# Attention over 25 blocks of query rows: each 125-row transposition split into halves of 64 and 61 rows, the two halves copied out by VectorE and ScalarE

## What is computed

```python
x = _layernorm(x + _L0_gnn_ref(x, ..., edge_weight, src, dst, edge_type_8), axis=-1)
x = _layernorm(x + _L1_gnn_ref(x, edge_index, ...), axis=-1)

def _transformer_conv(x, src, dst, Wq, bq, Wk, bk, Wv, bv, Ws, bs, heads):   # heads = 2, C = 64
    q = (x @ Wq + bq).reshape(n, heads, C)
    k = (x @ Wk + bk).reshape(n, heads, C)
    v = (x @ Wv + bv).reshape(n, heads, C)
    alpha = jnp.sum(q[dst] * k[src], axis=-1) / np.sqrt(C)
    ex = jnp.exp(alpha - amax[dst])                    # amax: segment maximum of alpha
    a = ex / denom[dst]                                # denom: segment sum of ex
    out = jax.ops.segment_sum(v[src] * a[..., None], dst, num_segments=n).reshape(n, heads * C)
    return out + x @ Ws + bs
# _L1_gnn_ref: conv with weights 1, ReLU, conv with weights 2
```

## Time and profile before

| | |
|---|---|
| median of 3 runs | 2248.33 us (2247.84 to 2248.36) |
| the profiled execution | 2249.5 us, of which the span of its instructions 2247.5 us |
| granted TensorE clock, mean over the span | 0.981 |
| TensorE matmul busy (PE) | 2104.2 us, 94% of the span |
| TensorE weight load busy (PEld) | 1707.9 us, 76% |
| VectorE (DVE) | 1590.5 us, 71% |
| ScalarE (ACT) | 1291.7 us, 57% |
| GpSimd (POOL) | 821.2 us, 37% |
| attention layer 1, steps | about 1250 to 1711 us |
| attention layer 2, steps | about 1762 to 2240 us |

### The profile page before, as it was taken

The page is one execution under the profiler, slowest core; times in us unless marked ns, Lnnn a source line. Parts: engine busy times, 40 slices in busy tenths (PEclk is TensorE's granted clock), DMA queues, the critical chain, the costliest instruction groups (busy, mean ns, idle before and its releaser), DMA issues. The chain is left out here.

```text
span 2247.5 us, 55086 instructions
## 1 busy us (share of the span) xinstructions
PE 2104.2 (94%) x19640; PEld 1707.9 (76%) x19640; DVE 1590.5 (71%) x4061; ACT 1291.7 (57%) x2303; POOL 821.2 (37%) x1091
## 2 busy tenths in 40 slices
PE   1299999999999999999997999999999999999998
PEld 1288888898888888888985677777776677777776
DVE  1458887888888888878873666666664666666765
ACT  1156666665666666666663555556564455565555
POOL 0766776777677667767710000000000000000000
PEclk9599999999999999999998999999999999999999
DMA  4001111111111111111112222222221122222220
GB/s 122 14 31 45 42 46 51 44 45 52 47 38 46 51 48 41 46 51 44 43 40 100 87 78 72 80 85 85 85 85 48 71 94 92 92 92 92 92 92 7
DMA packets 52538, 141.57 MB, mean 63 GB/s; under 512 B 9261, under 2 KB 43755, under 8 KB 45855
## 3 DMA queue, kind: packets, MB, share of 16 engines
q1 hardware_dynamic: 49804, 129.55, 16.3%
q0 software_dynamic: 2576, 9.68, 1.5%
HBM read 93.95 MB, written 45.27 MB: 62 GB/s over the span
## 5 line engine op out<-in xcount | busy, mean ns | idle before, releaser
L778 PE MATMUL ps<-matrixT,x_rows 125*128 125x256 f32 (+1 forms) x2500 | 582.7, 384 | 2.9 <-ACT aggT L864 2.1
L778 PEld LDWEIGHTS ps<-matrixT,x_rows 125*128 125x128 f32 x2500 | 461.4, 191 | 70.9 <-issue 3.3
L845 ACT COPY matrixT<-ps 125x500 f32<-125x500 f32 (+2 forms) x800 | 395.8, 583 | 201.5 <-PE ps L766 197.3
L1468 ACT COPY weightsT_l<-ps 125x500 f32<-125x500 f32 (+1 forms) x450 | 233.8, 542 | 369.2 <-PE ps L1389 369.2
L766 PE MATMUL ps<-high_weights,low_onehot 64*125 64x125 f32 x6300 | 403.8, 279 | 23.2 <-issue 11.3
L1546 DVE CUSTOM_DVE_ANT_0 scores_l<-ps,bias_rows_l 125x500 f32<-125x500 f32 (+1 forms) x700 | 396.8, 619 | 35.3 <-issue 33.7
L766 PEld LDWEIGHTS ps<-high_weights,low_onehot 64*125 64x125 f32 x6300 | 366.2, 189 | 54.0 <-issue 37.2
L1389 PEld LDWEIGHTS ps<-eye,scores_l 125*125 125x125 f32 x2500 | 301.1, 189 | 115.6 <-issue 97.2
L1389 PE MATMUL ps<-eye,scores_l 125*125 125x125 f32 x2500 | 364.2, 286 | 4.8 <-ACT scores_l L1450 3.4
L1554 DVE COPY weightsT_l<-ps 125x500 f32<-125x500 f32 (+1 forms) x250 | 150.0, 600 | 267.3 <-PE ps L1389 264.9
L1450 ACT ACTIVATE scores_l<-scores_l,neg_max_l 125x1500 f32<-125x1500 f32 x200 | 320.9, 1605 | 20.5 <-DVE neg_max_l L1583 20.4
(11 more groups left out here) (154 smaller groups left out, 1864.5 us busy)
## 6 DMA issues: line engine op xcount, KB each, us to landing
bias_rows_l<-bias SPq DMA_DIRECT2D x50, 1562.5 KB, 6.7
bias<-bias SPq DMA_DIRECT2D x150, 250.0 KB
edges<-rec POOLq DMA_DIRECT2D x1, 2014.2 KB, 11.8
x_rows<-in_x SPq DMA_DIRECT2D x1, 1562.5 KB
bias<-bias SPq DMA_DIRECT2D x25, 62.5 KB
x<-x_rows SPq DMA_DIRECT2D x25, 62.5 KB
x_rows_l<-x SPq DMA_DIRECT2D x25, 62.5 KB
out<-rows_l SPq DMA_DIRECT2D x25, 62.5 KB
```

Of the source, the lines that this page charges most:

```text
L778: last = nc.tensor.matmul(psG[:, BASES * SPLIT * side:BASES * (SPLIT * side + SIDE[side])], x[:, h, :], MT[side][:, 0:SIDE[side], BASES * ...
L845: last = nc.scalar.copy(MT[side][:, at:at + 2 * c - 1:2, 0:COLS], psP[bank][0:R, :].rearrange("p (i c) -> p i c", c=128)[:, 0:c, 0:COLS])
L1468: nc.scalar.copy(PT[i % 8][:, 0:cw[c]], psT[i % 2][0:R, 0:cw[c]]).then_inc(z["pa_ok"], 1)
```

## The change

- The operand of a turn is split by query rows: `QS = ((0, 64), (64, 125))`. Each square becomes two transpositions, one of partitions 0 to 63 into `psT[0]` and one of partitions 64 to 124 into `psT[1]`, both heads of the chunk in each bank.
- `turn(u, up, c)` now turns a whole chunk, both heads. It waits for both exps, and for both copies of the chunk before.
- The first half-square of each chunk is a plain matmul with the identity, not a transposition.
- The copies i = 2c (rows 0 to 63, ScalarE) and i = 2c + 1 (rows 64 to 124, VectorE) both start from the turned chunk: seven on each engine, where it was nine and five. `PT` is four tiles of a chunk each.
- The transposition of the sums and the skip product stand ahead of turn 2, not behind it.
- VectorE alternates masks and copies; `finish` stands behind mask 5; the copy of chunk 5 stands ahead of mask 6; in layer 2 the mean and variance (`moments`) come after the negated maximum and `normalize` a step later.

```diff
-        PT = [sb(f"weightsT{i}", [R, CW], F32) for i in range(8)]
+        PT = [sb(f"weightsT{i}", [R, HEADS, 4, R], F32) for i in range(4)]
-        ON_V = (1, 5, 8, 11, 13)
+        ON_V = (1, 3, 5, 7, 9, 11, 13)
+        QS = ((0, HD), (HD, R))
+        def turned_chunk(eng, u, i):
+
+            c, (lo, hi) = i // HEADS, QS[i % HEADS]
+            k = cw[c] // R
+            eng.wait_ge(z["t_ps"], u * CH + (c + 1))
+            buffer_free(eng, u, i)
+            return (PT[c % 4][:, :, 0:k, lo:hi],
+                    psT[i % HEADS][0:R, 0:HEADS * k * (hi - lo)].rearrange("p (h b q) -> p h b q", h=HEADS, b=k))
-            def turn(u, up, i):
-                c, hd = i // HEADS, i % HEADS
+            def turn(u, up, c):
+
                 if c in (0, EXP_AT):
-                    pe.wait_ge(z["exp_ok"], u * 4 + (hd + 1 + 2 * (c > 0)))
-
-                if i >= 2:
-                    chunk_out(pe, u, i - 2)
-                elif not is_int(u) or u >= 1:
-                    chunk_out(pe, u - 1, i - 2 + NT)
-                for b in range(cw[c] // R):
-                    n = 4 * c + b
-                    last = nc.tensor.transpose(psT[i % 2][0:R, b * R:(b + 1) * R], S[up][:, hd, n * R:(n + 1) * R],
-                                               eye[0:R, 0:R])
+                    pe.wait_ge(z["exp_ok"], u * 4 + (2 if c == 0 else 4))
+
+                for i in (HEADS * c - 2, HEADS * c - 1):
+                    if i >= 0:
+                        chunk_out(pe, u, i)
+                    elif not is_int(u) or u >= 1:
+                        chunk_out(pe, u - 1, i + NT)
+                k = cw[c] // R
+                for hd in range(HEADS):
+                    for b in range(k):
+                        at = (4 * c + b) * R
+                        for side, (lo, hi) in enumerate(QS):
+                            n = hi - lo
+                            to = psT[side][0:R, (hd * k + b) * n:(hd * k + b + 1) * n]
+                            if hd == 0 and b == 0 and side == 0:
+                                nc.tensor.matmul(to, S[up][lo:hi, hd, at:at + R], eye[lo:hi, lo:hi], start=True, stop=True)
+                            else:
+                                last = nc.tensor.transpose(to, S[up][lo:hi, hd, at:at + R], eye[lo:hi, lo:hi])
                 last.then_inc(z["t_ps"], 1)
...
+                if layer == 2 and inside(t - 3):
+                    normalize(t - 3, 1 - par)
                 if inside(t):
                     mask(2)
+                if inside(u):
+                    turned_out(3)
+                if inside(t):
                     mask(3)
                 if inside(u):
                     turned_out(5)
+                if inside(t):
+                    mask(4)
+                if inside(u):
+                    turned_out(7)
+                if inside(t):
+                    mask(5)
                 if inside(w):
                     finish(w, par, then)
-                if inside(t):
-                    mask(4)
-                    mask(5)
                 if inside(u):
-                    turned_out(8)
-                if layer == 2 and inside(w):
-                    normalize(w, par)
+                    turned_out(9)
+                    turned_out(11)
                 if inside(t):
                     mask(6)
...
                     V.tensor_scalar_mul(neg[par][:, :], top[:, :], -1.0).then_inc(z["neg_ok"], 1)
+                if layer == 2 and inside(w):
+                    moments(w, par, then)
                 if inside(u):
-                    turned_out(11)
                     turned_out(13)
```

More of the change, by code:

```diff
@@ L1362, in product @@
                         last = nc.tensor.matmul(psO[up][HD * hd:HD * (hd + 1), 0:R], vals[:, 4 * c + b, hd, :],
-                                                PT[(HEADS * c + hd) % 8][:, b * R:(b + 1) * R],
+                                                PT[c % 4][:, hd, b, :],
                                                 start=(c == 0 and b == 0), stop=(c == CH - 1 and b == 0))
@@ L1400, in step @@
                         product(w, par, CH - 1)
-                    if s > 0 and inside(u):
-                        turn(u, up, 4 * s - 4)
-                        turn(u, up, 4 * s - 3)
                     if s == 2 and inside(w):
@@ L1408, in step @@
                         nc.tensor.matmul(psO[par][0:R, 384:384 + D], x_now[par][:, :], W["s"][:, :], start=True, stop=True).then_inc(z["o_ps"], 1)
+                    if s > 0 and inside(u):
+                        turn(u, up, 2 * s - 2)
                     if s > 0 and inside(t):
@@ L1413, in step @@
                     if s > 0 and inside(u):
-                        turn(u, up, 4 * s - 2)
-                        turn(u, up, 4 * s - 1)
+                        turn(u, up, 2 * s - 1)
                         if s == 1 and (not is_int(u) or u >= 2):
@@ L1424, in step @@
                 if inside(u):
-                    turn(u, up, NT - 2)
-                    turn(u, up, NT - 1)
+                    turn(u, up, CH - 1)
             pipeline_loop(pe, step)
@@ L1464, in step @@
                             continue
-                        c = i // HEADS
-                        act.wait_ge(z["t_ps"], u * NT + (i + 1))
-                        buffer_free(act, u, i)
-                        nc.scalar.copy(PT[i % 8][:, 0:cw[c]], psT[i % 2][0:R, 0:cw[c]]).then_inc(z["pa_ok"], 1)
+                        to, turned_rows = turned_chunk(act, u, i)
+                        nc.scalar.copy(to, turned_rows).then_inc(z["pa_ok"], 1)
                         if layer == 1 and i == 12 and inside(w):
@@ L1513, in finish, with moments @@
                     V.tensor_scalar_max(r[:, :, :], r[:, :, :], 0.0).then_inc(z["rows_ok"], 1)
-                else:
-                    v.wait_ge(x_in[par], (half(w, par) + 1) * 16)
-                    then(V.tensor_tensor(r[:, :, :], r[:, :, :], x_old[par][:, :, :], ALU.add))
-                    then(V.bn_stats(stats[:, 0, :], r[:, 0, :]))
-                    V.memset(spare2[:, :], 0.0).then_inc(then.sem, 1)
-                    then.done = then.done + 1
-                    then(V.bn_aggr(mean[:, 0, :], stats[:, 0, :]))
-                    V.tensor_scalar_add(rstd[:, :, :], mean[:, :, 1:2], 1.0e-5).then_inc(z["asked"], 1)
+            def moments(w, par, then):
+                r = rows[par]
+                v.wait_ge(x_in[par], (half(w, par) + 1) * 16)
+                then(V.tensor_tensor(r[:, :, :], r[:, :, :], x_old[par][:, :, :], ALU.add))
+                then(V.bn_stats(stats[:, 0, :], r[:, 0, :]))
+                V.memset(spare2[:, :], 0.0).then_inc(then.sem, 1)
+                then.done = then.done + 1
+                then(V.bn_aggr(mean[:, 0, :], stats[:, 0, :]))
+                V.tensor_scalar_add(rstd[:, :, :], mean[:, :, 1:2], 1.0e-5).then_inc(z["asked"], 1)
             def normalize(w, par):
@@ L1537, in step @@
                     if not is_int(t) or t >= 2:
-                        v.wait_ge(z["t_ps"], (t - 1) * NT)
+                        v.wait_ge(z["t_ps"], (t - 1) * CH)
                         v.wait_ge(z["neg_ok"], t - 1)
@@ L1550, in turned_out @@
                 def turned_out(i):
-                    c = i // HEADS
-                    v.wait_ge(z["t_ps"], u * NT + (i + 1))
-                    buffer_free(v, u, i)
-                    V.tensor_copy(PT[i % 8][:, 0:cw[c]], psT[i % 2][0:R, 0:cw[c]]).then_inc(z["pt"], 1)
+                    to, turned_rows = turned_chunk(v, u, i)
+                    V.tensor_copy(to, turned_rows).then_inc(z["pt"], 1)
                 if inside(t):
@@ L1583, in step @@
                     V.tensor_scalar_mul(neg[par][:, :], top[:, :], -1.0).then_inc(z["neg_ok"], 1)
+                if layer == 2 and inside(w):
+                    moments(w, par, then)
                 if inside(u):
-                    turned_out(11)
                     turned_out(13)
-            pipeline_loop(v, step)
+            pipeline_loop(v, step, 2 if layer == 1 else 3)
 INPUTS = ['x', 'src', 'dst', 'edge_type_8', 'edge_weight', 'L0_gnn_V', 'L0_gnn_w_comp', 'L0_gnn_loop_w', 'L0_gnn_bias',
```

## The result

The changed kernel takes 2323.92 us (median of four runs, 2321.99 to 2325.05); the kernel before took 2248.35 us beside it. The ratio is 1.0334 (95% interval 1.0316 to 1.0352): 75.6 us slower. The profiled execution of the changed kernel took 2324.1 us with a span of 2322.1; its mean granted clock is 0.970, where it was 0.981. Two versions further down had one execution each that took far longer than their other three (2764.8 us in last_turns_apart, 5295.0 us in all_mended_whole_squares); no reading rests on these two.

A forecast was written before the change was run, and what follows sets the result against it. TensorE was taken as the bound, its work filling the attention step. Plain pass, saved switches and two waits summed to +58.7 us, making the profiled 2249.5 us 2308 and the median 2307; range 2255 to 2350 us, the forecast's own 2285 to 2335.

The forecast's parts named there:

- A half pair costs a whole square: In the turns, two half transpositions side by side take 0.109 us, as one whole square does; gain 0 us.
- Rivals 1 and 4: In turns: 1, streamed columns set the pace, 2190 us, 14%; 4, halves do not overlap, 2580 us, 4%.
- The plain pass: In each of seven chunks, the plain matmul's second pass costs one more load interval, +0.76 us a step.
- Rival 2: In the turns, the plain pass hides: 38 us less than forecast, 2269 us; chance 12%.
- Switches: On TensorE, fewer changes of array division at 0.195 us each: -0.98 us a step in layer 1, -1.17 in layer 2.
- rival 3: Between scores and turns the switch stays: +24 us, 2331 us; chance 7%.
- The wait at turn 5: Between turns 4 and 5, TensorE waits for both banks' copies under only the short chunk's scores, +0.82 us a step.
- The wait at turn 0: Ahead of turn 0, later exponentials (copy ahead of mask 6) hold TensorE: +0.62 us in layer 1, +0.77 in layer 2.
- The sum over the steps: Over both layers' steps, 29.9 us in layer 1 and 28.8 in layer 2, together +58.7 us.
- nothing but at the very end, below 1 us: At the kernel's end, the output's DMA going a step later costs below 1 us, elsewhere nothing.
- 1.9 us of scores or products cover the wait: Away from turn 5, scores or products stand under the wait for both banks' copies; edges costed at 0.

The follow-up runs named there:

- last_turns_apart: Changed kernel with a product between each two turns, from turn 1 on, in each layer's last step with turns; 2329.9 us.
- all_mended_whole_squares: all_mended with whole squares, one head in each bank, in place of the halves; 2266.7 us.
- no_plain: Changed kernel with each chunk's plain matmul made a transposition, the semaphore waits on an instruction of their own; 2295.6 us.
- whole_squares: Changed kernel with whole 125 x 125 squares, one head in each bank, in place of halves; order and waits kept; 2321.4 us.
- m6_first: Changed kernel with mask 6, the maximum and its negation ahead of VectorE's copy of chunk 5 again; 2297.3 us.
- last_step_whole: all_mended with the last step with turns of each layer turned in whole squares, other steps in halves; 2220.6 us.
- m6_first_no_plain: Changed kernel with both mask 6 ahead of the copy of chunk 5 and no plain matmul; 2264.2 us.
- scores5_later: Changed kernel with the scores of chunk 5 moved from behind turn 2 to behind turn 4; 2296.9 us.
- all_mended: Changed kernel with mask 6 first, no plain matmul, product 3 behind turn 4, earlier finish, and the last step of last_turns_apart; 2236.1 us.
- last_step_plain: all_mended with every half-square of each layer's last step turned by a plain two-pass matmul; 2252.9 us.

## Why the prediction was right, and where it was short

The direction was right and the time lay in the range: 2307 predicted, 2323.9 measured. By its own steps:

- **A half pair costs a whole square.** Right: 0.107 us a pair in the changed kernel, and sixteen halves in 0.95 us in no_plain. Rivals 1 and 4 fall, and with rival 1 the factor of two from the Trainium skill's page "TensorEngine Tiling (Array Packing)", section Theoretical Speedup: the moving columns fell from 125 to 64 and the pace stayed, which fits the prediction's reading that the loads of 125 columns set it.
- **The plain pass, +0.76 us a step.** Forecast 38 us in all; taking it out gave 28, 0.56 us a step. Over-sized by a quarter. The gain is that of five passes (5 x 0.109 = 0.55 us), and this fits the order: the other two stand ahead of a wait, turn 4's ahead of turn 5's (where no_plain gains nothing) and turn 6's ahead of turn 0's. Rival 2, that all of it hides, is out.
- **Switches, -0.98 and -1.17 us.** Right: the gap between halves and scores is gone, so rival 3 falls. The pair of mended versions measures 0.8 and 1.1 us a step; their order has two more switches than the changed one, with halves and with squares alike. In the changed order the saving was hardly seen (whole_squares), since the waits took it up.
- **The wait at turn 5, +0.82.** Right in size: turn 5 starts 2.08 us behind turn 4 in the trace (1874.73 to 1876.81), 2.02 were forecast. Spreading the scores gave 27 us back, not the 50 x 0.82 = 41 us of this term, since smaller waits came in its place.
- **The wait at turn 0, +0.62 and +0.77.** In layer 2 the loads there come 0.53 us later than before (0.89 against 0.36), so over-sized by 0.24; m6_first gave 27 us back, part of it at the layers' ends, where 33.4 were forecast. From turn 5 to turn 0 the trace has 6.15 us (1876.81 to 1882.96) and the forecast 6.40: it added the records' durations end to end, but the next instruction starts up to 0.1 us before the record ahead of it ends (VectorE's copy at 1878.05, 0.67 long, and mask 6 at 1878.64; the first exponential at 1879.58, and the copy behind it 1.54 us later, where 1.64 were counted).
- **The sum over the steps.** 58.7 us forecast; the steps and first intervals rose by 25.3 + 29.6 + 2.5 = 57.4. That these are so close is partly luck. An interval without a stretch at 1.2 GHz takes 20.36 us in layer 1 and 20.29 in layer 2 (means), 1.05 and 1.06 over the kernel before, where 1.22 and 1.18 were forecast; four steps with a stretch at 1.2 GHz, of which the forecast knew nothing, add 4.1 us.
- **What failed** is the sentence that the ends cost "nothing but at the very end, below 1 us", and with it the claim that 1.9 us of scores or products cover the wait for both banks everywhere but at turn 5. In the last step of a layer no scores are left. There turns 1, 3 and 5 each wait (0.97, 0.97 and 1.02 us of idle loads in layer 2, below), and the granted clock falls to 1.2 GHz in parts of it, so that the two products behind turn 3 take 3.12 us of loads where they take 1.77 in an ordinary step. That is +9.4 us at the end of layer 1 and +7.8 at that of layer 2, 17.2 us, about the whole difference between forecast and result (16.9). In the mended order the clock's share was shown by experiment: last_step_whole differs from all_mended by the shape of the squares in the last steps alone, and is 15.5 us faster. In the changed kernel itself waits and clock were not measured apart, since taking the waits away let the clock stay low for longer. What is known is that the same order in whole squares has 3.7 and 3.8 us less at the two ends (whole_squares): 7.5 of the 17.2 us go with the halves, their plain pass and their low clock, and 9.7 with the order.

```profile
2294.31 0.28 PEld L1406 LDWEIGHTS ps<-eye,scores_l 64*125 64x125 f32 x1 [0.97 <-ACT weightsT_l L1481]
...
2302.80 0.18 PEld L1406 LDWEIGHTS ps<-eye,scores_l 64*125 64x125 f32 x1 [0.97 <-issue]
...
2303.92 3.12 PEld L1372 LDWEIGHTS ps<-weightsT_l,values_l 125*64 125x64 f32 x32
...
2309.47 0.18 PEld L1406 LDWEIGHTS ps<-eye,scores_l 64*125 64x125 f32 x1 [1.02 <-ACT weightsT_l L1481]
```

Left open: the changed kernel's trace has four stretches at 1.2 GHz inside ordinary steps, here one of layer 1, which cost it 0.8 to 1.3 us each. The other traces narrow down where they come from. m6_first has four, no_plain three, m6_first_no_plain one and last_turns_apart five, and each of the 17 begins 0.9 to 1.3 us after the first load of a turn 5 that had to wait. The versions with halves but without that wait (scores5_later, all_mended and those made from it) have none, nor has whole_squares, which has the wait but no halves. That the two together set them off is not shown by an experiment made for it.

```profile
1532.60:1536.00 3.40, 3.40 (x33) 3.18 (x32) 1.43 (x8) 2.23 (x3) 0.00 (x0) 0.51 0.33 77
```

## What to carry to other kernels

Before an operand is split to fill the array, ask what sets the interval: here it was, by all that the rows show, the 125 stationary columns, which a split by rows leaves alone, and the gain was only that turns and scores share one division of the array (0.195 us a switch). A change that fills all buffers at once takes their double buffering away; go through every place where the next fill follows, the pipeline's last step too, where the work that covers it has run out. When two engines' orders are rewritten, find the chain that crosses into the next step (here maximum, two exponentials, turn 0) and keep everything that waits for a later event behind it.

## What the runs showed of the hardware that was not expected

TensorE's granted clock can stay at 1.2 GHz with the engine busy: 20.2 us of 20.2 in all_mended and 30.5 of 30.5 in last_step_plain, in stretches of turns by half-squares and products, without scores. In such a stretch sixteen half loads take 1.76 us instead of 0.95, and the loads of a product 1.54 instead of 0.84. With the last step in whole squares it was 2.4 GHz over 17 us with 2.9 of them idle (last_step_whole); with all steps in whole squares it fell in the last step and rose again (0.86 over 24 us in all_mended_whole_squares). In steps with 500-column scores between them, the same half-square turns ran at the full clock, all 431 us of layer 1 here:

```profile
1266.30:1697.60 431.30, 429.69 (x5337) 325.24 (x5335) 312.77 (x1150) 243.03 (x390) 12.11 (x46) 1.00 0.23 82
```

This line is of all_mended; the changed kernel, whose turn 5 waits, has the four short exceptions named above.
